# Quantising the MLP's hidden row in pieces inside the down-projection loop

## The reference, cut to what matters

```python
def _act_quant(x):
    scale = 127.0 / jnp.clip(jnp.max(jnp.abs(x), axis=-1, keepdims=True), 1e-05)
    xq = jnp.clip(jnp.round(x * scale), -128.0, 127.0) / scale
    return x + jax.lax.stop_gradient(xq - x)
def _bitlinear(x, w):
    return jnp.einsum('bsi,oi->bso', _act_quant(x), _weight_quant(w))
gate = jax.nn.silu(_bitlinear(x, w_gate))
up = _bitlinear(x, w_up)
return _bitlinear(gate * up, w_down)      # hidden width 4096, model width 1024
```

## Time and profile before

| | |
|---|---|
| median of 3 runs (lowest, highest) | 3863.93 us (3863.29, 3867.05) |
| profiled execution: its own time, its span | 3869.42 us, 3867.8 us |
| spans of the eight cores | 3837.0 to 3867.8 us |
| PE busy, share of the span, instructions | 1760.1 us, 46%, 8724 |
| DVE busy | 1414.1 us, 37%, 2405 |
| ACT busy | 976.7 us, 25%, 1164 |
| instructions of all engines; packets of the two instruction queues | 30557; 77 and 84 |

### The profile page before, as it was taken

One profiled execution on the slowest core, in us unless ns is written; L12 is line 12 of the kernel. 1 busy time (PEld: TensorE's weight loads), 2 busy tenths in 40 slices (PEclk: granted clock), 3 DMA queues, 4 the chain that ended last, 5 costly groups with the idle time before them and its releaser, 6 DMA issues.

```text
span 3867.8 us, 30557 instructions; the slowest of 8 cores (3837.0 to 3867.8 us)
## 1 busy us (share of the span) xinstructions
PE 1760.1 (46%) x8724; PEld 604.6 (16%) x8824; DVE 1414.1 (37%) x2405; ACT 976.7 (25%) x1164; POOL 18.7 (0%) x54
## 2 busy tenths in 40 slices
PE   1201112321034434565775776384466528472934
PEld 0000000100011111111111111132123213221411
DVE  1453474444455443323112112324224241604252
ACT  1202201220000115474785875010011001101100
POOL 1000000000000000000000000000000000000000
PEclk9999999955565555555555555696778769695958
DMA  5445353222410000101001000331242125022402
GB/s 114 163 158 179 138 188 93 70 77 76 156 40 11 0 11 6 39 1 44 1 1 44 1 1 17 114 112 33 74 131 68 59 69 153 25 84 90 131 24 82
DMA packets 140969, 278.28 MB, mean 72 GB/s; under 512 B 7944, under 2 KB 106504, under 8 KB 134664
## 3 DMA queue, kind: packets, MB, share of 16 engines
q1 hardware_dynamic: 107256, 192.96, 15.3%
q10 hardware_dynamic: 24320, 67.12, 5.1%
q0 software_dynamic: 9232, 16.25, 2.7%
HBM read 250.61 MB, written 41.94 MB: 76 GB/s over the span
## 4 chain that ended last, share of the span: by engine, by line
PE 20%; DVE 16%; ACT 14%; DMA 7%; issue 5%; DVEq 1%; ACTq 0%; SPq 0%
PE ps_f L1062 6%; PE ps_f L1068 6%; DMA wdbuf<-scr_d 4%; PE ps_f L1149 4%; ACT PTb L730 4%; ACT PTb L734 4%; ACT PT L730 3%; ACT PT L734 3%; DVE xsc L1092 2%; PE ps_tf L958 1%; DMA xo_t<-xo 1%; DVE den_sb L808 1%; DVE hbuf L1104 1%; DVE hq L1112 1%; DVE hbuf L1108 1%
## 5 line engine op out<-in xcount | busy, mean ns | idle before, releaser
L706 PE MATMUL ps_sc<-qn,khat 32*128 32x512 bf16 (+3 forms) x1280 | 313.5, 530 | 134.7 <-ACT PT L730 48.6
L1149 PE MATMUL ps_f<-wdbuf,hqT 128*128 128x512 bf16 x1000 | 257.0, 405 | 101.4 <-DMA wdbuf<-scr_d 74.6
L1062 PE MATMUL ps_f<-wgbuf,xqT 128*128 128x512 bf16 x1005 | 246.0, 386 | 120.3 <-DMA wubuf<-scr_u 118.1
L1068 PE MATMUL ps_f<-wubuf,xqT 128*128 128x512 bf16 x1002 | 241.4, 381 | 1.3 <-issue 0.2
L1082 DVE SCALAR_TENSOR_TENSOR hbuf<-ps_f,xsc,gate_s 128x512 f32<-128x512 f32 x128 | 96.0, 750 | 398.4 <-ACT gate_s L1076 398.4
L742 DVE TENSOR_TENSOR PT<-PT,maskD 128x512 bf16<-128x512 bf16 x64 | 27.2, 425 | 489.1 <-ACT PT L734 489.1
L730 ACT ACTIVATE PT<-ps_sc,negMb 128x1024 bf16<-128x1024 f32 (+3 forms) x160 | 157.8, 986 | 121.2 <-PE ps_sc L706 108.8
L958 PE MATMUL ps_tf<-ident,hq 128*128 128x128 bf16 x512 | 71.7, 301 | 229.1 <-DVE hq L1112 214.5
L1076 ACT ACTIVATE gate_s<-ps_f,xsc 128x512 f32<-128x512 f32 x128 | 88.0, 687 | 344.6 <-PE ps_f L1068 344.6
L353 PE MATMUL ps_tr<-ident,xst 128*128 128x128 bf16 x384 | 52.2, 304 | 267.4 <-DVE xTc L29 178.0
L730 ACT ACTIVATE PTb<-ps_sc,negMb 128x1024 bf16<-128x1024 f32 (+3 forms) x160 | 157.8, 986 | 35.9 <-PE ps_sc L706 24.6
(11 more groups left out here) (223 smaller groups left out, 2442.5 us busy)
## 6 DMA issues: line engine op xcount, KB each, us to landing
wgbuf<-scr_g SPq DMA_DIRECT2D x32, 1024.0 KB, 7.5
wubuf<-scr_u SPq DMA_DIRECT2D x32, 1024.0 KB, 10.4
wfbuf<-wgT SPq DMA_DIRECT2D x8, 2048.0 KB, 10.0
wfbuf<-wgT ACTq DMA_DIRECT2D x8, 2048.0 KB, 8.6
wfbuf<-wuT SPq DMA_DIRECT2D x8, 2048.0 KB, 13.0
wfbuf<-wuT ACTq DMA_DIRECT2D x8, 2048.0 KB, 9.9
wfbuf<-wdT SPq DMA_DIRECT2D x32, 512.0 KB, 3.6
wfbuf<-wdT ACTq DMA_DIRECT2D x32, 512.0 KB, 4.1
```

Of the source, the lines that this page charges most:

```text
L706: e.matmul(ps_sc[:, j * 512 + stc:j * 512 + 512], khat[32 * j:32 * j + 32, gi * T + sc * 128: gi * T + sc * 128 + 128], qn[32 * j:32 * j + 32,
L1062: P.emit(t, lambda e, c=c, i4=i4, bi=bi, gb=gb: e.matmul(ps_f[:, gb:gb + 512], xqT[:, i4 * D + c * 128:i4 * D + c * 128 + 128], wgbuf[bi][ ...
L1068: P.emit(t, lambda e, c=c, i4=i4, bi=bi, ub=ub: e.matmul(ps_f[:, ub:ub + 512], xqT[:, i4 * D + c * 128:i4 * D + c * 128 + 128], wubuf[bi][ ...
L1149: e.matmul(ps_f[:, ((2 + i4) % 4) * 512: ((2 + i4) % 4) * 512 + 512], hqT[:, i4 * INNER + io * 128: i4 * INNER + io * 128 + 128], wdbuf[bi ...
```

## The change

The row maximum is now built up during gate/up: after each product DVE reduces the 512 new columns, and takes the larger of that and the maximum so far. The 4096-column reduce goes. The quantising stage keeps only its one-column operations. The three passes, the transposes and the copies move into the first half of the down-projection: before each even step the 512 columns that this step and the next need are quantised, for all four row groups. `hq` is used in four quarters, one per row group, and the copy goes to DVE for even row groups and to ACT for odd ones. PE's wait for all of DVE and ACT stands before each even step of the first half.

```diff
@@ gate/up, after the product into hbuf
+                            if io == 0:
+                                P.emit(v, lambda e, i4=i4, io=io, c8=c8:
+                                       e.tensor_reduce(
+                                           xsc[:, c8 + 5:c8 + 6],
+                                           hbuf[:, i4 * INNER + io * 512:
+                                                i4 * INNER + io * 512 + 512],
+                                           AX, ALU.max, apply_absolute_value=True))
+                            else:
+                                P.emit(v, lambda e, i4=i4, io=io: e.tensor_reduce(
+                                    sm[:, 9:10],
+                                    hbuf[:, i4 * INNER + io * 512:
+                                         i4 * INNER + io * 512 + 512],
+                                    AX, ALU.max, apply_absolute_value=True))
+                                P.emit(v, lambda e, c8=c8: e.tensor_max(
+                                    xsc[:, c8 + 5:c8 + 6], xsc[:, c8 + 5:c8 + 6],
+                                    sm[:, 9:10]))
@@ quantising stage
-                        P.emit(v, lambda e, i4=i4, c8=c8: e.tensor_reduce(
-                            xsc[:, c8 + 5:c8 + 6],
-                            hbuf[:, i4 * INNER:(i4 + 1) * INNER], AX, ALU.max,
-                            apply_absolute_value=True))
...
-                        P.emit(v, lambda e, i4=i4, c8=c8: e.tensor_scalar(
-                            hbuf[:, i4 * INNER:(i4 + 1) * INNER],
-                            hbuf[:, i4 * INNER:(i4 + 1) * INNER],
-                            xsc[:, c8 + 6:c8 + 7], MAGIC, ALU.mult, ALU.add))
...
-                        mk_hq = P.emit(v, lambda e, i4=i4: e.tensor_scalar_max(
-                            hq[:], hbuf[:, i4 * INNER:(i4 + 1) * INNER], -128.0),
-                            waits=[(cT, cT.v)], incs=[(cV, 1)])
-                        for b in range(8):
-                            srcs = [hq[:, (4 * b + k) * 128:(4 * b + k) * 128 + 128]
-                                    for k in range(4)]
-                            ftr_batch(srcs,
...
-                                      [(cV, mk_hq[1])] if b == 0 else [], b % 2)
@@ down-projection, at the head of a step
+                            if fh == 0 and ic % 2 == 0:
+                                b8 = ic // 2
+                                for i4 in range(4):
+                                    c8 = 8 * i4
+                                    hs = i4 * INNER + b8 * 512
+                                    P.emit(v, lambda e, hs=hs, c8=c8: e.tensor_scalar(
+                                        hbuf[:, hs:hs + 512], hbuf[:, hs:hs + 512],
+                                        xsc[:, c8 + 6:c8 + 7], MAGIC,
+                                        ALU.mult, ALU.add))
+                                    P.emit(v, lambda e, hs=hs: e.tensor_scalar(
+                                        hbuf[:, hs:hs + 512], hbuf[:, hs:hs + 512],
+                                        MAGIC, 127.0, ALU.subtract, ALU.min))
+                                    mk_hq = P.emit(v, lambda e, i4=i4, hs=hs:
+                                                   e.tensor_scalar_max(
+                                                       hq[:, i4 * 512:i4 * 512 + 512],
+                                                       hbuf[:, hs:hs + 512], -128.0),
+                                                   waits=[(cT, cT.v)],
+                                                   incs=[(cV, 1)])
+                                    srcs = [hq[:, i4 * 512 + k * 128:
+                                               i4 * 512 + k * 128 + 128]
+                                            for k in range(4)]
+                                    ftr_batch(srcs,
+                                              (lambda i4, b8: lambda e, psl: _cp(e,
+                                                  hqT[:, i4 * INNER + b8 * 512:
+                                                      i4 * INNER + b8 * 512 + 512],
+                                                  psl[:, 0:512]))(i4, b8),
+                                              [(cV, mk_hq[1])], i4 % 2)
@@ down-projection, the waits of a matmul
-                                    if io == 0 and i4 == 0:
+                                    if (i4 == 0 and sub == 0 and fh == 0
+                                            and ic % 2 == 0):
                                         w.append((cV, cV.v))
                                         w.append((cA, cA.v))
+                                    if io == 0 and i4 == 0:
+                                        if fh == 1:
+                                            w.append((cV, cV.v))
+                                            w.append((cA, cA.v))
                                         if mk_dev is not None:
                                             w.append(mk_dev)
```

More of the change, by code:

```diff
@@ L1102, in build_nc @@
                         P.emit(v, lambda e, c8=c8: e.tensor_scalar_mul(
-                            xsc[:, c8 + 7:c8 + 8], xsc[:, c8 + 5:c8 + 6], 1.0 / 127.0))
-                        P.emit(v, lambda e, i4=i4, c8=c8: e.tensor_scalar(
-                            hbuf[:, i4 * INNER:(i4 + 1) * INNER],
-                            hbuf[:, i4 * INNER:(i4 + 1) * INNER],
-                            xsc[:, c8 + 6:c8 + 7], MAGIC, ALU.mult, ALU.add))
[L1108 to L1111, removed]
-                        mk_hq = P.emit(v, lambda e, i4=i4: e.tensor_scalar_max(
-                            hq[:], hbuf[:, i4 * INNER:(i4 + 1) * INNER], -128.0),
-                            waits=[(cT, cT.v)], incs=[(cV, 1)])
-                        for b in range(8):
-                            srcs = [hq[:, (4 * b + k) * 128:(4 * b + k) * 128 + 128]
-                                    for k in range(4)]
-                            ftr_batch(srcs,
[L1119 to L1122, removed]
-                                      [(cV, mk_hq[1])] if b == 0 else [], b % 2)
+                            xsc[:, c8 + 7:c8 + 8], xsc[:, c8 + 5:c8 + 6],
+                            1.0 / 127.0), incs=[(cV, 1)])
                     mk_dev = None
```

## The result

The changed kernel takes 3936.56 us, median of 8 runs (3931.55 to 3956.7), against 3867.01 us for the kernel before (8 runs, 3862.97 to 3872.3). The ratio is 1.0187, 95% interval 1.0169 to 1.0205: 1.9% slower. The forecast was 3918 us, range 3880 to 3967. The loss is 69.5 us where 54 were forecast.

The account below looks back on a forecast made before the run. Alternating DVE and PE work bounds the quantising stage. 6.3 us plus eight rounds, 124 us, make 130.3 against 117.2 us a tile: +52.5 over four, plus 1 fetching; 3869.4 + 54 - 5.5 = 3918 us, range 3880 to 3967.

Parts of the forecast that it names:

- Reductions hidden: Gate/up: short row-maximum reduces run under matmuls, costing only 1.06 us a tile; four 4.42 us reduces leave the quantising path.
- Cost of short passes: DVE, 512 columns: quantising passes 427 us/1000 plain, 485 ns with a scale column; row-maximum reduces 686 ns.
- rival of cheap passes: Quantising pieces: passes at the copy's 294 ns plus 58 for the scale column, 43 us saved, 3875 us; chance 0.05.
- The round is serial: First down-projection half: quantising, transposes, copies and matmuls run in sequence, 15.5 us a round, eight rounds a tile.
- The part ahead of the matmuls: Each down-projection round: exposed passes, gaps, hand-overs and copies before its matmuls, 10.18 us.
- The burst: Each round's 16 down-projection matmuls start at the low clock: 5.5 us, less 0.2 us for transposes still at high clock.
- case of wholly cold bursts: Down-projection rounds: all 16 matmuls at 1.2 GHz, 7.04 us a burst, 17.2 us a round, 3972 us; chance 0.08.
- The base: Kernel before: last gate/up product to first down half's end, 117.2 us a tile, with the slowest core standing for all.
- the 1 us added for instruction fetching: Whole kernel: about 560 more DVE instructions bring a little fetching, taken as 1 us.
- The weight loads: Down-projection rounds: loads land in 2.8 us; the odd one, on ACT, lands at 12.3 us, hidden before even matmuls end.
- The 0.5 us a round worked out for a fast PE: Down-projection rounds: with a fast PE, even matmuls end at 11.3 us and wait about 0.5 us for the odd load.
- some 20 us: Matmul part before the change: weight-load waits that go, already in the sum because rounds are built from new.

## Why the prediction was right, point by point

**Reductions hidden.** Right: -66.5 us measured alone, -68 worked out; no time in gate/up.

**Cost of short passes.** Right: 486, 427 and 685 ns against 485, 427 and 686. The rival of cheap passes falls.

**The round is serial.** Right, and shown from two sides. With the pass's wait narrowed only 36 us come back; with the queues reordered and the loads on SP the round falls to DVE's own work.

**The part ahead of the matmuls.** Right: 9.97 us in the round shown and 10.08 on average, 9.98 in the sum.

**The burst.** Right in kind, undersized: 5.76 us on average for the 5.5 taken, 0.26 x 32 = 8 us. I took the mean of bursts after the pause between halves, which is 5.56 us in the trace, nearer 5.6 than 5.5. The new rounds leave PE less to do ahead of a burst than either stage of before; that this is why was argued, not tested. Keeping the clock up was worth 55 us in the run that kept PE busy. The case of wholly cold bursts falls, the longest of 224 being 6.57 us against 7.04. In every one of the 256 bursts the first matmuls stand about 0.43 us apart, as at the low clock, for 5 to 14 of them. By this the rule of the Trainium skill ("TensorE: Matmul & The Clock Gate", section "HAM oscillation") held for how a burst starts, not for how it ends.

**The base.** This term was off by as much as the burst. I took 117.2 us from the slowest core. The average over the eight cores was 115.1, and the other seven had averages of 114.6 to 115.1. That is 2.1 x 4 = 8 us. The quantising part was as long on that core as on the others (74.6 us for 74.3 to 74.6); the excess lay in the matmul part, 42.7 us at a granted clock of 0.92, where the others had 40.3 to 40.9 us at 0.95 or 0.96. The sentence that the slowest core stands for all was wrong by this much.

**Together.** 54 + 8 + 8 = 70 us; 69.5 were measured. The forecast of 54 was thus short by 15 us, and both errors pointed the same way. Of the 1 us added for instruction fetching no run shows anything: the stretches alone account for 71 us.

**The weight loads.** Right: hidden while PE is slow. The 0.5 us a round worked out for a fast PE is the wait seen in the run that kept it busy, 0.47 us on average. But the "some 20 us" of weight-load waits in the first half before was twice too much: the trace has 8.9 us a tile. It stood in no sum.

## What to carry to other kernels

Moving work into a loop overlaps nothing unless the order of each queue lets it: write down, for one iteration, what each engine's next instruction waits for, and see whether anything runs beside the matmuls. Emitting the producer one iteration ahead turned +70 us into -200 us with the same passes, transposes and matmuls (the copies all on ACT, the loads all on SP). The clock came back in the same step, from 0.64 to 0.88 in the stretch, as PE's idle time between bursts went. When such an order is changed, every DMA issue that shares a queue with the moved work moves too, and must be counted. And take the base of a sum from all cores, not from the slowest.

## What the runs showed of the hardware

A DMA issue on ACT's queue goes out when the copy ahead of it starts, not when it ends (2655.39 and 2655.46 us in the round above), but no earlier; behind a copy that waits for another engine it waits as well. Moving these issues to SP took 140 us off here. And 26 matmuls a round whose result nobody reads made the kernel 55 us faster by holding the granted clock at 0.95 instead of 0.64.
